# A relation-weighted graph network: the combination bases in chunks of 120 rows instead of 128

## The chip, the cores and the metric

The kernel runs on one core of a Trainium2 chip. The metric is the device time in microseconds of one execution; three runs of the kernel before gave 996.9, 996.52 and 996.86 us, a median of 996.86. One further execution was taken with the hardware profiler.

## The reference, cut to what matters

The whole program is two blocks of a network over 625 nodes with 512 features: graph convolution plus linear attention, then a mixture of experts, then the same again with other layers. The change touches one part only, the weights of the first block's two gated relational convolutions:

```
w = einsum('rb,bio->rio', att, basis)      # r = 2 relations, b = 30 bases, i = o = 512
msg_r = (gate_r * x[col]) @ w[r]           # then chosen by edge type and summed per node
h   = relu(layer1(x)); out = layer2(h)     # each layer has its own basis (30 x 512 x 512) and att (2 x 30)
```

The two bases are 2 x 30 x 512 x 512 fp32 numbers, 62.9 MB. Every output row `w[r, i, :]` is a sum over 30 rows `basis[b, i, :]` with the coefficients `att[r, b]`.

## The kernel before, in words

**The combination.** On the host the bases are laid out in 16 groups (8 for each layer). A group is 64 input rows i: four quarters of 16. For each i the 30 bases follow one another, so a group is 64 x 30 = 1920 rows of 512 numbers, 15 chunks of 128 rows. TensorE multiplies a chunk with a matrix `Am` whose entries are att where a row belongs to the wanted i, and zero elsewhere; the result is 32 rows of 512 (16 values of i for each of two relations), written to one of four quarters of the PSUM bank `CB` (`CB[32 * j:32 * j + 32]`). A quarter is 480 rows, which is 3.75 chunks of 128, so three of the chunks (3, 7 and 11) belong to two quarters and are multiplied twice: 18 products for 15 chunks. `PARTS` lists them as (chunk, quarter), in an order in which four successive ones go to four quarters; `ORDER` is the order of the chunks in memory. Products are fp32.

**The ring.** The 240 chunks come as 80 loads of three chunks (128 rows x 6144 bytes), five loads per group, into seven buffers. SyncE issues them in order (`load_basis`): load n waits until load n-5 has landed and until TensorE has given back the buffer of load n-7. TensorE gives back a buffer after the products number 2, 5, 8, 11 and 17 of a group (`FREES`, semaphore `combo_done`). All loads go through SyncE's one queue.

**The order of the work.** On TensorE a group of products is a call of `combos(n)`. Group 0 and 1 come first, between small products and transposes; then 24 steps of one-hot products follow (`SEGS`, line 497), which count the edges per pair of nodes, with groups 2 to 13 after every second step (`AFTER`); their inputs are made by DVE and ScalarE two steps ahead. After them TensorE computes the root products of layer 1 (line 509), then group 14, a small product that DVE turns into a flag (`many`), and group 15. ScalarE (`combo_out`, even groups) and DVE (`combo_in`, odd groups) take `CB` out to the weights `W`; `combos` waits for that (`w_ready`). Then the stage with the products of line 549 begins, which needs the rounded matrices `Dr` from ScalarE and `GXl` from DVE. When the last group is done, SyncE starts the loads of the next weights (`Wqkv`, `R1`, `R2`).

**Am.** DVE builds it at the start with six operations at line 1226 from a 0/1 mask and att, both loaded before everything else.

Of the kernel before, what the change touches and what calls it, by code (L numbers as in the profile page):

```python
# [29 lines left out]

PARTS = ((0, 0), (4, 1), (8, 2), (12, 3), (1, 0), (5, 1), (9, 2), (13, 3), (2, 0), (6, 1), (10, 2), (14, 3),
         (3, 0), (3, 1), (11, 2), (11, 3), (7, 1), (7, 2))
ORDER = (0, 4, 8, 12, 1, 5, 9, 13, 2, 6, 10, 14, 3, 11, 7)
FREES = (2, 5, 8, 11, 17)
SLOTS = 7

AFTER = [g // 2 + 2 if g % 2 else None for g in range(NS)]
FLUSHES = (NS + PER - 1) // PER  # L40
# [82 lines left out]
def build(nc, A, out):  # L123
    ctx = ExitStack()
    with ctx:
        def sb(name, shape, dt=F32):
            return ctx.enter_context(nc.sbuf_tensor(name, shape, dt))

        def sem(name):
            return ctx.enter_context(nc.semaphore(name))  # L130
# [49 lines left out]
        spare = sb("spare", [128, 3072])  # L180
# [8 lines left out]
        def ar(off, *dims, p=128):  # L189
            n = 1  # L190
            for d in dims:
                n *= d
            v = AR[0:p, off:off + n]
            if len(dims) == 1:
                return v
            names = "abcdefgh"[:len(dims)]
            return v.rearrange("p (%s) -> p %s" % (" ".join(names), " ".join(names)),
                               **{k: d for k, d in zip(names, dims)})

        def sl(i, a, b, p=128):  # L200
            return PS[0:p, i * 1024 + a:i * 1024 + b]
# [9 lines left out]
        def wide(f, o):  # L211
# [6 lines left out]
        oXN, oXT, oG, oZ, oW1, oW2, oR2, oRING, oA, oOT, oB = (  # L218
            0, 2560, 5120, 10240, 15440, 19536, 23632, 25680, 31824, 33872, 40496)
# [12 lines left out]
        W = [ar(oW1, 2, 4, 512), ar(oW2, 2, 4, 512)]  # L232


        Am = ar(oA, 2, 18, 48)
        amask, att = ar(oW2, 18, 16), ar(oW2 + 512, 18, 2, 2)
        ring = [ar(oR2 + 1536 * i, 3, 512) for i in range(5)] + [
            spare[:, 1536 * i:1536 * i + 1536].rearrange("p (c n) -> p c n", c=3) for i in range(2)]
        ei = ar(oOT, 3, EP).bitcast(I32)
        ef = ar(oB + 1024, 3, EP, p=P)  # L240
        ge_ = ar(oOT + 512, NT + 1, EP, p=P)
# [21 lines left out]

        gw = [ar(oB, 2, 512), ar(oB - 374, 2, 512)]
        bias2, bias_out = ar(oB + 512, 512, p=P), ar(oB, 512, p=P)
        R1, R1e = ar(oA, 4, 512), [ar(o, 512) for o in (14720, oRING + 5632, oW2 + 1536, oW2 + 3584)]
        R2 = ar(oR2, 4, 512)
        Wqkv = ar(oRING, 4, 1536)
        WO = ar(oW1 + 2048, 4, 512)
# [1 line left out]
        CB = PS[:, 3584:4096]  # L271
# [9 lines left out]
        d_ring = [sem("d_ring%d" % i) for i in range(5)]  # L281
# [10 lines left out]
        combo_done, seg_done = sem("combo_done"), sem("seg_done")  # L292
# [106 lines left out]
        def _(te):  # L399
            pe = Waits(te)  # L400
# [34 lines left out]
                ins.then_inc(u.sem, 1)  # L435


            def combos(n, a=0, b=len(PARTS)):
                l = n // 8
                pe.wait_ge(w_ready, n)  # L440
                for m, (c, j) in list(enumerate(PARTS))[a:b]:
                    at = ORDER.index(c)
                    pe.wait_ge(d_ring[at // 3], 16 * (n + 1))
                    held = ring[(5 * n + at // 3) % SLOTS]
                    quarter = [k for k, part in enumerate(PARTS) if part[1] == j]
                    ins = te.matmul(CB[32 * j:32 * j + 32, :], Am[:, l, m, 16 * (n % 2):16 * (n % 2) + 32],  # L446
                                    held[:, at % 3, :], start=m == quarter[0], stop=m == quarter[-1])
                    if m in FREES:
                        ins.then_inc(combo_done, 1)

            psum.held.add(3)
            pe.wait_ge(am_ready, 6)
# [26 lines left out]
            for g, (u, v) in enumerate(SEGS):  # L479
# [3 lines left out]
                if first:  # L483
                    for k in range(7):
                        if g:
                            pe.wait_ge(flush_done, NT * (g // PER - 1) + min(NT, (512 * k + 511) // N + 1))
                        te.matmul(PS[0:P, k * 512:(k + 1) * 512], low[0:1, 0:P], low[0:1, 128:640],
                                  start=True, stop=False, skip_group_check=True)
# [3 lines left out]
                for b in range(NT):  # L492
                    with te.If_ne(regs[b], 0):
                        for t in range(u, v):
                            for blk, p0, p1 in PIECES:
                                if blk == b:
                                    te.matmul(PS[0:P, p0:p1], oh_dst(g, t)[:, cols(b)], oh_src(g, t)[:, p0 - b * N:p1 - b * N],  # L497
                                              start=False, stop=False, skip_group_check=True)
# [20 lines left out]
                pe.wait_ge(s, v)  # L519
            for c in range(4):  # L520
                root1(c, bank[c])
            combos(14, 0, 12)
            u = psum.take("many", "dve", slot=2)
            slot(u)
            pe.wait_ge(many_ready, 1)
            te.matmul(sl(u.slot, 0, 10, 1), ones[0:P, 0:1], sm[0:P, 3, 0:2, 0:5], start=True, stop=True).then_inc(u.sem, 1)
            combos(14, 12)
            combos(15)
            psum.at = 2
            psum.held.discard(3)  # L530
# [134 lines left out]
            for c in range(NT):  # L665
                u = psum.take(("l2", c), "dve", slot=c // 2 if c < 4 else None, keep=c in (1, 3))
                o = bank[c] if c < 4 else sl(u.slot, 0, 512, P)
# [60 lines left out]
            for c in range(NT):  # L728
                ins = te.transpose(sl(1, c * P, (c + 1) * P, 8) if c < 4 else sl(1, 512, 512 + P, 8), M[:, c, :], ident[0:P, 0:P])
# [152 lines left out]
            for c in range(NT):  # L882
                read(psum["a1", c])
                o = c * P if c < 4 else 512
                ins = te.transpose(sl(u.slot, o, o + P), x1r[0:P, c, :], ident[0:P, 0:P])
            ins.then_inc(u.sem, 1)
            read(psum["KV", 1, 1])
            for c in range(NT):
# [50 lines left out]
            for c in range(NT):  # L939
                ins = te.matmul(sl(u.slot, c, c + 1, P), x1a[:, cols(c)], wa[:, 1, 0:1], start=True, stop=True)  # L940
# [3 lines left out]
            for c in range(NT):  # L944
                ins = te.transpose(sl(u.slot, c * 128, c * 128 + 128, P), x1a[:, cols(c)], ident[:, :])
# [158 lines left out]
            ins = logits2(4)  # L1104
# [48 lines left out]
        def _(ve):  # L1153
            dv = Waits(ve)
# [68 lines left out]
            dv.wait_ge(d_att, 32)  # L1223
            for lay in range(2):
                for k in range(3):
                    ve.tensor_tensor(Am[:, lay, :, 16 * k:16 * k + 16], amask,
                                     att[:, :, lay, k % 2].unsqueeze(2).to_broadcast([128, 18, 16]),
                                     ALU.mult).then_inc(am_ready, 1)
            dv.wait_ge(d_edge, 16)
            ve.tensor_scalar(nsrc, ei[0:P, 0, :], -STEEP, STEEP / 2, ALU.mult, ALU.add).then_inc(nsrc_ready, 1)  # L1230
# [28 lines left out]
            for i, (b0, b1) in enumerate(((0, 3), (3, 5))):  # L1259
                k = full(("cnt", i))  # L1260
# [24 lines left out]
            def combo_in(k):  # L1285

                l, kc = k // 8, k % 8 // 2
                dv.wait_ge(combo_done, 5 * (k + 1))
                dv.wait_ge(w_ready, k)
                for r in range(2):  # L1290
                    ins = ve.scalar_tensor_tensor(out=W[l][:, r, kc, :], in0=CB, scalar=halves[1 - r], in1=W[l][:, r, kc, :],
                                                  op0=ALU.mult, op1=ALU.add)
                ins.then_inc(w_ready, 1)
# [69 lines left out]
            i = full("many")  # L1363
# [166 lines left out]
            i = full("place", 1)  # L1530
# [22 lines left out]
            for c in range(NT):  # L1553
                ins = ve.tensor_scalar(dgk[:, c, :], ident[0:P, 0:P], key[0:P, c:c + 1], None, ALU.mult)
# [5 lines left out]
            for k in (1, 3):  # L1560
                i = full(("xs", k))
# [3 lines left out]
            i = full("krow")  # L1565
# [208 lines left out]
            for c in range(NT):  # L1774
                i = full(("mo", c))
# [123 lines left out]
            for j in range(2):  # L1899
                i = full(("tp", j))  # L1900
# [31 lines left out]
            for c in range(NT):  # L1932
                i = full(("out", c))
# [4 lines left out]
        def _(se):  # L1938
            ac = Waits(se)
# [45 lines left out]
            def combo_out(k):  # L1985

                l, kc = k // 8, k % 8 // 2
                ac.wait_ge(d_cst, 16)
                ac.wait_ge(combo_done, 5 * (k + 1))
                for r in range(2):  # L1990
                    ins = copy(W[l][:, r, kc, :], CB, scale=halves[r])
                ins.then_inc(w_ready, 1)
# [122 lines left out]
            for k in (0, 2):  # L2115
                i = full(("xs", k))
# [4 lines left out]
            i = full("MT")  # L2121
# [85 lines left out]
            i = full("xt4")  # L2207
# [67 lines left out]
            i = full("x1n")  # L2275
# [187 lines left out]
        def _(ye):  # L2463
            sp = Waits(ye)
# [14 lines left out]
            ye.dma_start(iota[:, :], A["c_iota"]).then_inc(d_iota, 16)  # L2479

            def load_basis(n):
                r = n % 5
                if n >= 5:
                    sp.wait_ge(d_ring[r], 16 * (n // 5))
                if n >= SLOTS:
                    sp.wait_ge(combo_done, n - SLOTS + 1)
                ye.dma_start(ring[n % SLOTS], A["basis"][n]).then_inc(d_ring[r], 16)

            ye.dma_start(X[:, :, :], A["x"].rearrange("c p f -> p c f")).then_inc(d_x, 16)
            ye.dma_start(cst[:, :], A["c_cst"]).then_inc(d_cst, 16)  # L2490
            for n in range(5):
                load_basis(n)
            def load_gates(lay, d):
                ye.dma_start(gw[lay][0:P, :, :].rearrange("p r i -> p (r i)"), A["gate_w"][lay:lay + 1, :].to_broadcast([P, 1024])).then_inc(d, 16)

            load_gates(0, d_gw0)
            for n in range(5, 80):
                load_basis(n)
                if n == 32:
                    for k in range(4):  # L2500
                        ye.dma_start(R1e[k], A["L0_gnn_root1"][128 * k:128 * k + 128, :]).then_inc(d_r1e, 16)
                if n == 40:
                    sp.wait_ge(gl_ready, NT)
                    ye.dma_start(bias1, A["bias1"]).then_inc(d_bias, 16)
                    ye.dma_start(bias2, row(A["L0_gnn_bias2"]).to_broadcast([P, 512])).then_inc(d_bias2, 16)
            sp.wait_ge(combo_done, 80)
            ye.dma_start(Wqkv, kp(A["L0_mix_W_qkv"])).then_inc(d_wqkv, 16)
            ye.dma_start(R1, kp(A["L0_gnn_root1"])).then_inc(d_r1, 16)
            ye.dma_start(R2, kp(A["L0_gnn_root2"])).then_inc(d_r2, 16)
# [157 lines left out]
```

## Time and profile before

| | |
|---|---|
| median of three runs | 996.86 us |
| the profiled execution, its own time | 994.57 us |
| the span of that execution | 992.8 us |
| TensorE matmul busy | 934.3 us, 94% of the span |
| DVE busy | 557.6 us, 56% |
| ScalarE busy | 401.1 us, 40% |
| mean granted TensorE clock | 0.984 of full speed |
| bytes moved by DMA | 124.87 MB, of which 62.9 MB are the bases |

Times in the profile are microseconds from the start of the span unless marked ns. PE is TensorE's matmul part and PEld its weight load part, which overlap; SPq is SyncE's DMA queue. An fp32 product shows as two records. "DMA share" is the mean busy share of the core's 16 DMA engines.

### The profile page before, as it was taken

The page shows a single profiled execution, that of the slowest core. Times are in us where ns is not written, and L with a number is a line of the kernel's source. Part 1 is how long each engine was busy: PE and PEld are TensorE (multiplying, and loading weights), DVE is VectorE, ACT ScalarE, POOL GpSimd, SP SyncE. Part 2 cuts the span into 40 slices and gives each one's busy share as a digit, 9 for nine tenths or more (in the row PEclk, how much of TensorE's full clock was granted, in tenths as well). Part 3 has the DMA queues.
Part 4 walks back from the last instruction along what each step waited for, and adds up shares of the span by engine and source line. Part 5 has one row for each costly group of instructions (what it writes and reads, how often), then busy time and mean ns, then how long its engine had stood idle before and what let it go on. Part 6 is the DMA issues. An engine that isn't in the chain of part 4 may idle for free. (4 is left out here: it accounts for less than half of the span.)

```text
span 992.8 us, 12505 instructions
## 1 busy us (share of the span) xinstructions
PE 934.3 (94%) x4724; PEld 610.9 (62%) x4724; DVE 557.6 (56%) x1176; ACT 401.1 (40%) x670; POOL 109.5 (11%) x98
## 2 busy tenths in 40 slices
PE   3989889999999999999998999989999899999997
PEld 0445444395454494468765656989997644545885
DVE  4798888823147611441315662697876533658861
ACT  3677777311102210111112333478785543424450
POOL 0000000000020213100002000144340000023300
PEclk9999999999999999989999999999999999999899
DMA  9999989560000101062985203222103100230001
GB/s 299 380 392 358 380 332 366 207 218 0 1 21 1 54 20 67 0 223 95 308 288 188 81 1 97 78 64 66 43 1 120 51 1 3 89 85 0 1 1 52
DMA packets 53086, 124.87 MB, mean 126 GB/s; under 512 B 5455, under 2 KB 19539, under 8 KB 53010
## 3 DMA queue, kind: packets, MB, share of 16 engines
q1 hardware_dynamic: 51890, 122.51, 34.6%
q0 software_dynamic: 1120, 1.29, 0.4%
q8 instruction: 56, 0.92, 0.4%
q14 instruction: 20, 0.16, 0.0%
HBM read 120.40 MB, written 3.38 MB: 125 GB/s over the span
## 5 line engine op out<-in xcount | busy, mean ns | idle before, releaser
L412 PE MATMUL PS<-AR 128*125 128x512 f32 (+9 forms) x1394 | 393.9, 440 | 9.0 <-issue 1.9
L412 PEld LDWEIGHTS PS<-AR 128*128 128x128 f32 (+3 forms) x1394 | 212.5, 194 | 168.9 <-issue 161.9
L1951 ACT ACTIVATE AR<-PS 128x500 f32<-128x500 f32 (+6 forms) x73 | 41.9, 578 | 162.4 <-PE PS L412 81.2
L1954 ACT ACTIVATE AR<-iota,AR 125x625 f16<-125x625 f16 x119 | 86.3, 811 | 27.8 <-PE PS L499 27.7
L446 PE MATMUL PS<-AR 128*32 128x512 f32 x420 | 68.1, 628 | 20.8 <-DMA AR<-in_basis 20.5
L1279 DVE TENSOR_SCALAR AR<-iota,AR 125x625 f16<-125x625 f16 x165 | 60.5, 446 | 13.8 <-PE PS L499 13.8
L497 PE MATMUL PS<-AR 125*125 125x512 f16 (+9 forms) x425 | 59.8, 297 | 4.5 <-issue 3.7
L497 PEld LDWEIGHTS PS<-AR 125*125 125x125 f16 x425 | 45.0, 139 | 22.7 <-issue 13.5
L2447 POOL TENSOR_TENSOR whl<-AR,whh 128x512 fp32r<-128x512 f32 x32 | 47.3, 1499 | 90.3 <-ACT whh L1951 90.3
L1799 DVE TENSOR_TENSOR HMl<-AR,HMh 128x626 fp32r<-128x626 f32 x64 | 50.6, 830 | 4.3 <-ACT HMh L1951 4.3
L446 PEld LDWEIGHTS PS<-AR 128*32 128x32 f32 x420 | 15.3, 112 | 57.3 <-issue 39.7
L1951 ACT ACTIVATE HMh<-AR 128x626 fp32r<-128x626 f32 x64 | 43.2, 729 | 13.2 <-DVE AR L1794 13.2
L1954 ACT ACTIVATE sd<-mv,eps 125x1 f32<-125x1 f32 x35 | 10.3, 297 | 94.1 <-DVE mv L1175 86.9
L549 PE MATMUL PS<-Dr,GXh 125*128 125x314 f32 (+1 forms) x160 | 46.7, 310 | 0.0
L549 PE MATMUL PS<-Dr,GXl 125*128 125x314 f32 (+1 forms) x160 | 46.2, 307 | 0.0
L1954 ACT ACTIVATE AR<-PS,bh 128x626 f32<-128x626 f32 (+1 forms) x48 | 35.8, 780 | 18.8 <-PE PS L412 18.7
L1390 DVE TENSOR_SCALAR AR<-PS 125x512 f32<-125x512 f32 (+1 forms) x18 | 13.3, 742 | 50.8 <-PE PS L412 50.8
L412 PE MATMUL PS<-HMh,whh 128*128 128x314 f32 (+1 forms) x128 | 39.8, 311 | 1.8 <-ACT AR L1954 1.5
L412 PE MATMUL PS<-x1h,whh 128*128 128x314 f32 (+1 forms) x128 | 40.1, 313 | 1.1 <-DVE AR L1794 0.8
L412 PE MATMUL PS<-x1h,whl 128*128 128x314 f32 (+1 forms) x128 | 40.1, 313 | 0.0
L412 PE MATMUL PS<-x1l,whh 128*128 128x314 f32 (+1 forms) x128 | 39.4, 308 | 0.0
L412 PE MATMUL PS<-HMl,whh 128*128 128x314 f32 (+1 forms) x128 | 39.3, 307 | 0.0
(320 smaller groups left out, 1512.1 us busy)
## 6 DMA issues: line engine op xcount, KB each, us to landing
AR<-in_basis SPq DMA_DIRECT2D x58, 768.0 KB, 9.4
AR<-in_L_ffn_W SPq DMA_DIRECT2D x20, 1024.0 KB, 7.8
spare<-in_basis SPq DMA_DIRECT2D x22, 768.0 KB, 9.4
AR<-in_L_gnn_Wh SPq DMA_DIRECT2D x8, 512.0 KB, 4.0
AR<-in_L_gnn_Wh SPq DMA_DIRECT2D x16, 256.0 KB, 4.7
AR<-in_L_mix_W_qkv SPq DMA_DIRECT2D x1, 3072.0 KB, 11.4
AR<-in_L_gnn_root SPq DMA_DIRECT2D x2, 1024.0 KB, 14.7
y_dram<-AR SPq DMA_DIRECT2D x8, 256.0 KB, 8.4
```

Source lines behind the costliest of these rows:

```text
L412: ins = te.matmul(o, l, r, start=start and i == 0, stop=stop and i == len(pairs) - 1)
L446: ins = te.matmul(CB[32 * j:32 * j + 32, :], Am[:, l, m, 16 * (n % 2):16 * (n % 2) + 32], held[:, at % 3, :], start=m == quarter[0], stop= ...
L497: te.matmul(PS[0:P, p0:p1], oh_dst(g, t)[:, cols(b)], oh_src(g, t)[:, p0 - b * N:p1 - b * N], start=False, stop=False, skip_group_check=True)
L549: ins = te.matmul(o, w, Dr[r][0:P, d, a:b], **z)
L1279: ve.tensor_scalar(oh_dst(g, t)[:, 0:N], iota[0:P, 0:N], ef[:, 1, t:t + 1], ef[:, 2, t:t + 1], ALU.is_equal, ALU.mult).then_inc(dst_ready, 1)
L1390: ve.tensor_scalar(t, i, 0.0, None, ALU.min).then_inc(phi_min, 1)
L1799: ve.tensor_tensor(HMl[q][:, f, :], tmp[f], f32(HMh[q][:, f, :]), ALU.subtract).then_inc(hm_lo, 1)
L1951: return se.activation(o, i, ACT.Copy, scale=scale)
L1954: return se.activation(o, i, f, bias=bias, scale=scale)
L2447: ge.tensor_tensor(lo[:, ks], v, f32(hi[:, ks]), ALU.subtract).then_inc(pool_wl, 1)
```

## The change

A chunk becomes 120 rows, four values of i with their 30 bases. A quarter is then exactly four chunks, and a group 16 chunks and 16 products, none of them double. A load brings four chunks, one for each quarter: 120 rows of 8192 bytes in SBUF, read from memory as two blocks of 120 rows x 4096 bytes. There are 64 loads, four per group, and five buffers. `Am` has one block of 48 columns per position of the chunk in its quarter (4 instead of 18). Semaphores: one `d_ring` for each buffer, `combo_done` counts four per group, and a load waits only for its buffer. The extra load of `R1e` is issued after load 26 instead of 32, the one of the bias after load 32 instead of 40; one tile of `R1e` moves into what the ring leaves free in `spare`.

```diff
-PARTS = ((0, 0), (4, 1), (8, 2), (12, 3), (1, 0), (5, 1), (9, 2), (13, 3), (2, 0), (6, 1), (10, 2), (14, 3),
-         (3, 0), (3, 1), (11, 2), (11, 3), (7, 1), (7, 2))
-ORDER = (0, 4, 8, 12, 1, 5, 9, 13, 2, 6, 10, 14, 3, 11, 7)
-FREES = (2, 5, 8, 11, 17)
-SLOTS = 7
+ROWS = 120
+LOADS = 64
+SLOTS = 5
...
-        Am = ar(oA, 2, 18, 48)
-        amask, att = ar(oW2, 18, 16), ar(oW2 + 512, 18, 2, 2)
-        ring = [ar(oR2 + 1536 * i, 3, 512) for i in range(5)] + [
-            spare[:, 1536 * i:1536 * i + 1536].rearrange("p (c n) -> p c n", c=3) for i in range(2)]
+        Am = ar(oA, 2, 4, 48, p=ROWS)
+        amask, att = ar(oW2, 4, 16, p=ROWS), ar(oW2 + 512, 2, 2, p=ROWS)
+        ring = [ar(oR2 + 2048 * i, 4, 512, p=ROWS) for i in range(4)] + [
+            spare[0:ROWS, 0:2048].rearrange("p (c n) -> p c n", c=4)]
...
-            def combos(n, a=0, b=len(PARTS)):
+            def combos(n, a=0, b=4):
                 l = n // 8
                 pe.wait_ge(w_ready, n)
-                for m, (c, j) in list(enumerate(PARTS))[a:b]:
-                    at = ORDER.index(c)
-                    pe.wait_ge(d_ring[at // 3], 16 * (n + 1))
-                    held = ring[(5 * n + at // 3) % SLOTS]
-                    quarter = [k for k, part in enumerate(PARTS) if part[1] == j]
-                    ins = te.matmul(CB[32 * j:32 * j + 32, :], Am[:, l, m, 16 * (n % 2):16 * (n % 2) + 32],
-                                    held[:, at % 3, :], start=m == quarter[0], stop=m == quarter[-1])
-                    if m in FREES:
-                        ins.then_inc(combo_done, 1)
+                for j in range(a, b):
+                    m = 4 * n + j
+                    pe.wait_ge(d_ring[m % SLOTS], 16 * (m // SLOTS + 1))
+                    for q in range(4):
+                        ins = te.matmul(CB[32 * q:32 * q + 32, :], Am[:, l, j, 16 * (n % 2):16 * (n % 2) + 32],
+                                        ring[m % SLOTS][:, q, :], start=j == 0, stop=j == 3)
+                    ins.then_inc(combo_done, 1)
...
-                    ve.tensor_tensor(Am[:, lay, :, 16 * k:16 * k + 16], amask,
-                                     att[:, :, lay, k % 2].unsqueeze(2).to_broadcast([128, 18, 16]),
+                    ve.tensor_scalar(Am[:, lay, :, 16 * k:16 * k + 16], amask, att[:, lay, k % 2:k % 2 + 1], None,
                                      ALU.mult).then_inc(am_ready, 1)
...
             def load_basis(n):
-                r = n % 5
-                if n >= 5:
-                    sp.wait_ge(d_ring[r], 16 * (n // 5))
+                r = n % SLOTS
                 if n >= SLOTS:
                     sp.wait_ge(combo_done, n - SLOTS + 1)
-                ye.dma_start(ring[n % SLOTS], A["basis"][n]).then_inc(d_ring[r], 16)
+                ye.dma_start(ring[r].rearrange("p (h c) n -> p h c n", h=2), A["basis"][n].rearrange("h p c n -> p h c n")).then_inc(d_ring[r], 16)
```

## Rows read from the trace of the kernel before

**Rows 1.** The page, busy tenths of 40 equal slices of the span.
```profile
PE   3989889999999999999998999989999899999997
...
DMA  9999989560000101062985203222103100230001
```

**Rows 2.** DMA issues of the whole execution: count, KB each, median us to landing.
```profile
AR<-in_basis SPq DMA_DIRECT2D x58, 768.0 KB, 9.4
...
spare<-in_basis SPq DMA_DIRECT2D x22, 768.0 KB, 9.4
```

**Rows 3.** Windows: length, busy us of each engine, clock, DMA share, GB/s.
```profile
12.00:36.00 24.00, 17.97 (x84) 5.18 (x84) 14.79 (x44) 9.51 (x16) 0.00 (x0) 0.86 1.02 368
36.00:72.00 36.00, 33.10 (x238) 16.39 (x238) 30.89 (x85) 25.81 (x38) 0.00 (x0) 1.00 0.98 383
72.00:84.00 12.00, 10.36 (x77) 6.04 (x77) 11.34 (x32) 9.31 (x14) 0.00 (x0) 1.00 0.76 300
84.00:144.00 60.00, 54.04 (x389) 30.21 (x388) 50.44 (x121) 45.71 (x66) 0.00 (x0) 0.97 1.01 391
144.00:156.00 12.00, 11.76 (x102) 6.74 (x101) 10.73 (x26) 8.38 (x12) 0.00 (x0) 1.00 0.58 211
156.00:180.00 24.00, 23.41 (x143) 10.43 (x142) 21.12 (x37) 15.90 (x26) 0.00 (x0) 1.00 1.01 400
180.00:192.00 12.00, 10.63 (x62) 3.47 (x65) 10.95 (x30) 2.37 (x5) 0.00 (x0) 1.00 0.45 153
...
168.00:180.00 12.00, 11.47 (x41) 4.43 (x34) 12.00 (x18) 7.40 (x13) 0.00 (x0) 1.00 1.00 413
```

**Rows 4.** TensorE's timeline: start, us, work, idle before it, releaser.
```profile
14.38 5.37 PE L446 MATMUL PS<-AR 128*32 128x512 f32 x18 [14.38 <-DMA AR<-in_basis]
...
23.72 1.94 PE L446 MATMUL PS<-AR 128*32 128x512 f32 x8 [2.31 <-DMA AR<-in_basis]
...
36.56 1.92 PE L446 MATMUL PS<-AR 128*32 128x512 f32 x12 [0.83 <-DMA AR<-in_basis]
...
101.09 1.92 PE L446 MATMUL PS<-AR 128*32 128x512 f32 x12 [0.82 <-DMA AR<-in_basis]
...
171.17 13.97 PE L509 MATMUL PS<-AR 128*125 128x512 f32 x32 [0.21 <-DVE AR L1329]
...
190.95 1.48 PE L446 MATMUL PS<-spare,AR 128*32 128x512 f32 x10 [1.37 <-ACT AR L1951]
...
195.59 1.92 PE L446 MATMUL PS<-AR 128*32 128x512 f32 x12 [0.80 <-DMA AR<-in_basis]
197.44 0.42 PE L549 MATMUL PS<-Dr,GXh 125*128 125x314 f32 x1
```

**Rows 5.** Timeline of SyncE's queue, then of ScalarE, before 198 us.
```profile
186.22 2.01 SPq L2487 DMA_DIRECT2D AR<-in_basis  x3
...
191.30 6.25 ACT L1951 ACTIVATE Dr<-AR 125x626 fp32r<-125x626 f32 x10
```

**Rows 6.** Timeline of TensorE in group 3: a weight load, the products.
```profile
54.75 0.15 PEld L446 LDWEIGHTS PS<-AR 128*32 128x32 f32 x4 [0.27 <-issue]
...
54.32 2.78 PE L446 MATMUL PS<-AR 128*32 128x512 f32 x24 [0.34 <-issue]
56.90 1.92 PE L446 MATMUL PS<-spare,AR 128*32 128x512 f32 x12
```

**Rows 7.** Windows: the last three loads; the second gate load.
```profile
187.00:195.00 8.00, 6.40 (x46) 1.28 (x38) 6.16 (x15) 5.37 (x10) 0.00 (x0) 1.00 0.83 296
281.00:284.00 3.00, 3.00 (x29) 3.00 (x28) 2.14 (x9) 0.00 (x0) 0.00 (x0) 1.00 0.32 130
```

**Rows 8.** TensorE's waits, 36 to 198 us; one in its timeline.
```profile
PE PS L446 <- DMA AR<-in_basis: 2.7, 4, 0.8
...
PE PS L446 <- DMA spare<-in_basis: 0.3, 1, 0.3
...
130.29 2.09 PE L497 MATMUL PS<-AR 125*125 125x173 f16 x14 [2.28 <-issue]
```

More of the change, by code:

```diff
@@ L265, in build @@
         bias2, bias_out = ar(oB + 512, 512, p=P), ar(oB, 512, p=P)
-        R1, R1e = ar(oA, 4, 512), [ar(o, 512) for o in (14720, oRING + 5632, oW2 + 1536, oW2 + 3584)]
+        R1, R1e = ar(oA, 4, 512), [
+            ar(14720, 512), spare[:, 2048:2560], ar(oW2 + 1536, 512), ar(oW2 + 3584, 512)]
         R2 = ar(oR2, 4, 512)
@@ L521, in _ @@
                 root1(c, bank[c])
-            combos(14, 0, 12)
+            combos(14, 0, 3)
             u = psum.take("many", "dve", slot=2)
@@ L526, in _ @@
             te.matmul(sl(u.slot, 0, 10, 1), ones[0:P, 0:1], sm[0:P, 3, 0:2, 0:5], start=True, stop=True).then_inc(u.sem, 1)
-            combos(14, 12)
+            combos(14, 3)
             combos(15)
@@ L1287, in combo_in @@
                 l, kc = k // 8, k % 8 // 2
-                dv.wait_ge(combo_done, 5 * (k + 1))
+                dv.wait_ge(combo_done, 4 * (k + 1))
                 dv.wait_ge(w_ready, k)
@@ L1988, in combo_out @@
                 ac.wait_ge(d_cst, 16)
-                ac.wait_ge(combo_done, 5 * (k + 1))
+                ac.wait_ge(combo_done, 4 * (k + 1))
                 for r in range(2):
@@ L2481, in load_basis @@
             def load_basis(n):
-                r = n % 5
-                if n >= 5:
-                    sp.wait_ge(d_ring[r], 16 * (n // 5))
+                r = n % SLOTS
                 if n >= SLOTS:
                     sp.wait_ge(combo_done, n - SLOTS + 1)
-                ye.dma_start(ring[n % SLOTS], A["basis"][n]).then_inc(d_ring[r], 16)
+                ye.dma_start(ring[r].rearrange("p (h c) n -> p h c n", h=2), A["basis"][n].rearrange("h p c n -> p h c n")).then_inc(d_ring[r], 16)
             ye.dma_start(X[:, :, :], A["x"].rearrange("c p f -> p c f")).then_inc(d_x, 16)
             ye.dma_start(cst[:, :], A["c_cst"]).then_inc(d_cst, 16)
-            for n in range(5):
+            for n in range(SLOTS):
                 load_basis(n)
@@ L2496, in _ @@
             load_gates(0, d_gw0)
-            for n in range(5, 80):
+            for n in range(SLOTS, LOADS):
                 load_basis(n)
-                if n == 32:
+                if n == 26:
                     for k in range(4):
                         ye.dma_start(R1e[k], A["L0_gnn_root1"][128 * k:128 * k + 128, :]).then_inc(d_r1e, 16)
-                if n == 40:
+                if n == 32:
                     sp.wait_ge(gl_ready, NT)
@@ L2505, in _ @@
                     ye.dma_start(bias2, row(A["L0_gnn_bias2"]).to_broadcast([P, 512])).then_inc(d_bias2, 16)
-            sp.wait_ge(combo_done, 80)
+            sp.wait_ge(combo_done, LOADS)
             ye.dma_start(Wqkv, kp(A["L0_mix_W_qkv"])).then_inc(d_wqkv, 16)
@@ L2631 @@
     a["basis"] = np.stack([g["L0_gnn_basis1"], g["L0_gnn_basis2"]])[:, :, group].transpose(0, 2, 3, 1, 4).reshape(
-        16, 15, 128, 512)[:, list(ORDER)].reshape(80, 3, 128, 512).transpose(0, 2, 1, 3)
-    flat = 128 * np.array([c for c, _ in PARTS])[None, :] + np.arange(128)[:, None]
-    a["att"] = np.stack([g["L0_gnn_att1"], g["L0_gnn_att2"]])[:, :, flat % 30].transpose(2, 3, 0, 1)
-    a["c_amask"] = (flat[:, :, None] // 30 == np.arange(16) + 16 * np.array([j for _, j in PARTS])[:, None]).astype(np.float32)
+        16, 2, 2, 4, ROWS, 512).transpose(0, 3, 1, 4, 2, 5).reshape(LOADS, 2, ROWS, 2, 512)
+    rows = np.arange(ROWS)
+    a["att"] = np.stack([g["L0_gnn_att1"], g["L0_gnn_att2"]])[:, :, rows % 30].transpose(2, 0, 1)
+    a["c_amask"] = (4 * np.arange(4)[:, None] + rows[:, None, None] // 30 == np.arange(16)).astype(np.float32)
     a["gate_w"] = np.stack([g["L0_gnn_gate_w1"], g["L0_gnn_gate_w2"]]).reshape(2, 1024)
```

## Prediction

> **What bounds the kernel now.** I read the page's 40 slices first, then the DMA share by stage, then TensorE's own timeline of the stage the change touches, then SyncE's. The reader is to see in [rows 1] that TensorE is busy nearly everywhere, and that in the first eight slices (some 198 us), unlike the rest, the DMA engines are full too. That stage reads the 62.9 MB of bases (80 loads of 768 KB, [rows 2]) while TensorE works through 16 groups of combination products, with the one-hot products between them. [Rows 3] is the ledger of that stage: between 36 and 180 us the 16 engines are full in all but two stretches, at 383 to 400 GB/s, 392 in the mean; the free time is 24% of 12 us around 78 us (2.9 us) and 42% of 12 us around 150 us (5.0 us). Both are places where the ring was full because TensorE came late to a group. So the stage stands on two legs of nearly one length: TensorE alone would need little less, the DMA engines alone would need 7.9 us less. [Rows 4] show which leg carries: TensorE stood still for a load in groups 1, 7, 13 and 15 (0.83, 0.82, 0.3 and 0.80 us, that of group 13 in [rows 8]). In these four groups a later load is a later end, one for one. After 197.44 us the next stage starts at once on TensorE, and what else it needs is there: the rounding of Dr began at 191.30 and was at its tenth and last tile at the end [rows 4, 5]. A shift at 197 us goes through to the end.
>
> **The change, part by part.**
>
> *Products.* A group now has 18 products in five rounds; those of a round lie in different quarters of the output and run side by side. [Rows 6]: weight loads come four at a time every 0.43 us, twice per product (fp32 is recorded as two), so a round is 0.86 us whatever its number of products, and a group is 10 x 0.43 = 4.3 us (54.32 to 58.82 with its ends, 4.5). After the change it is four rounds of four: 3.44 us. That is 0.86 us less TensorE work per group, 13.8 us over sixteen. Rows 120 instead of 128 deep don't change a pass. Whether it counts is the loads' matter.
>
> *Loads.* 80 x 786,432 bytes become 64 x 983,040: the same 62.9 MB. What changes is who carries them. A load to 128 rows keeps 16 engines full [rows 3]. The nearest row for another number of rows is the second gate load, 125 rows of 4096 bytes, alone on the queue: a DMA share of 0.32 at 130 GB/s [rows 7]. That is five engines of 16 (5/16 = 0.31), each at 130/5 = 26 GB/s. 125 rows are five times 25. I take it that the rows are dealt in equal shares to at most 16 engines, so 120 rows go to 15 engines, eight rows each, and one stands idle.
> The Trainium skill says the same ("DMA: Bandwidth & Descriptors", section "Why a DMA increments its semaphore by 16 and not by 1"): the number of engines is the largest one up to 16 that divides the slowest dimension of both sides, 10 for 100 partitions. By that rule it is 15 for 120. It speaks against this change, and this trace agrees for 125 rows.
> Packet size: 26 GB/s per engine at 4096 bytes stands beside 413/16 = 25.8 at 6144 bytes in the fullest stretch (168 to 180 us, [rows 3]). I cost the smaller packets at nothing; at most 2% of the stream (3 us) if their fixed part is paid more often, and 3 us less if 15 engines meet fewer delays than 16 (392 is 95% of 413). So 62.9 MB take 62.9/392 = 160.5 us now and 171.2 us at 15/16 of it: +10.7 us, bounds +7 and +14. Up to group 13, 14 of 16 groups: +9.4 us (6 to 12).
>
> *Ring.* Now 7 buffers of 3 chunks, 21 chunks of 128 rows (5.5 MB); then 5 of 4, 20 of 120 rows (4.9 MB). The 0.6 MB that can't be held ahead are 1.5 us of the stream: of the 7.9 us of free DMA time some 6 us remain to soak up the slower stream (bounds 3 and 7.9). In its place the last load of a group releases less work: now two rounds follow it (1.85 us from the last wait, 195.59 to 197.44, [rows 4]), then one (0.86): -1.0 us.
> Up to the end of group 13: 9.4 - 6.0 - 1.0 = +2.4 us.
>
> *End of the stage.* Between groups 13 and 14 TensorE has 13.97 us of root products [rows 4]; meanwhile the ring fills and the queue stands (share 0.45 from 180 to 192, [rows 3]). The time from there is set by what can't be in the ring yet. Now 7 of the last 10 loads are in it and three follow; the first is issued at 186.22, a round after group 14 began [rows 5]; data flow in the 8 us from 187 at 296 GB/s, 2.37 MB [rows 7], and the last product pair waits until 195.59. After: five of eight are in the ring, and three of 0.98 MB follow, 2.95 MB. At 296 x 16/15 us per byte: 8.0 x 1.25 x 1.067 = 10.7 us against 8.0, +2.7 by this row; of the 8 us one is start and end, so I take 2.35. The last rounds save 0.9. Together +1.45 us (bounds +0.5, +2.5). The wait of 1.37 us for ACT between groups 14 and 15 [rows 4] lies before this and is covered: group 14 ends 0.86 earlier, and TensorE waits for loads instead.
>
> *Small edits.* Am is built by six DVE operations, which shrink from 288 elements to 64; but the first product waits for its load, until 14.38 [rows 4], not for them: nothing. The mask and att loads shrink with them. The five first loads go out with no wait, 4.9 MB instead of 3.9, and the gate load behind them lands later, which some 0.5 us of the bounds hold; the first group only needs the first load, 0.2 MB longer: 0.5 us, part of the stream. R1e's second tile moves to another place, and the loads at n = 26 and 32 stand at the same byte of the stream as 32 and 40 did. 32 fewer products are 128 fewer records of 12,505: nothing.
>
> **Sum.** +2.4 + 1.45 = +3.85 us. TensorE also lost 2.3 us before 130.29 to neither a load nor an engine that the profile names [rows 8]; arriving later, it may lose less of such time. I take 0.4 off: +3.4 us. The profiled span goes from 992.8 to 996.2, its own time from 994.57 to 998.0; the shown runs have a median 2.3 us above that one (996.86), so the median goes to **1000.3 us**. Its own range, by the bounds (+7 instead of +10.7 in the stream and all 7.9 us soaked up; +14 and 3 us): 997 to 1007.
>
> **Rivals.**
> *A, the loads keep all 16 engines (or 15 move as much).* 64 loads of 240 packets deal evenly, 15 to an engine, if packets and not rows are dealt; and 15 x 26 = 390 GB/s is what 16 reach now with their delays. Against it: the 125-row load has 125 packets, and its five engines don't tell rows from packets; but it shows that uneven counts are not dealt to 16. Then the shorter groups count: 12 x 0.86 = 10.3 us for TensorE in groups 2 to 13, of which the stream gives no more than its free 7.9, less some 2 for the smaller ring: -6. At the end 0.59 MB more after the ring (+2.0) and 0.9 less work: +1. Together -5: 992 us, at best 989. This is the side of faster.
> *B, the slack is wider than I think.* TensorE waited for loads in only 2.7 + 0.3 us after 36 us [rows 8]. If the free time soaks up all (7.9) and the stream loses but 7, group 13 ends 1 to 2 us earlier and the end gives it back: 0 to +2, 997 to 999 us.
> *C, the 15 engines get in one another's way.* With eight rows in a row each, two engines may come to write the same part of the memory at once; 128 rows on 16 engines evidently don't (25.8 GB/s each). If such pairs share one engine's rate half of the time, the stream of 171 us becomes 1.5 times as long: +85 us less 6 of slack, some 1080 us; if all the time, 1165. It decides as soon as the rate falls below 360 GB/s. For it speaks nothing in this trace; against it, five engines at full rate with 125 rows [rows 7], but few engines rarely meet.
> The Trainium skill ("SBUF — State Buffer", section "Door 1: The DMA port swizzle (why `[64,N]` ≈ `[32,N]`)") has partitions 32 apart behind one port, each port at one engine's rate; by it engines e and e+4 would meet. No row here shows it.
> *D, TensorE's clock.* After a wait of 2.31 us before 23.72 [rows 4] the granted clock was lower (0.86 in the mean of 12 to 36 us, [rows 3], so partly at 1.2 instead of 2.4 GHz). More waits for loads may bring more of it; while loads set the pace it costs nothing, and 1 to 2 us at most in the groups that TensorE sets. It widens the range only.
>
> **How the numbers follow.** The forecast case +1.5 to +10 has 0.52; A 0.22; B 0.14; C 0.12. 0.2% is 2.0 us, about what a measurement of this kernel tells from no change. Faster: A, and a little of B: 0.24. Same: most of B and the low end of the forecast: 0.20. Slower: 0.56. The range from 990 to 1008 us holds A, B and nearly all of the forecast; C is left out.
>
> **What would show it.** The DMA share in the full stretches falls to 0.94 (15/16) and GB/s to about 365 to 370; packets of 4096 bytes, and L446 with 512 records. TensorE's L446 rounds: 8 steps of 0.43 us per group when all is there. The waits of L446 for loads rise from 3 us after 36 us to about 15, one before the last round in most groups; the DMA share around 78 and 150 us rises. Next stage from 197.44 to about 200.8. A share of 1.0 at 390 GB/s and a stage end near 192 is A; a share of 0.94 with 200 to 300 GB/s is C. Wrong in another way I would be if the stages after 197 us changed their length by more than 1 us.

## The result, and the profile after

| | before | after |
|---|---|---|
| median | 996.69 us (4 runs, 993.92 to 996.9) | 1098.56 us (4 runs, 1098.06 to 1111.89) |
| the profiled execution, its own time | 994.57 us | 1098.57 us |
| its span | 992.8 us | 1096.8 us |
| mean granted TensorE clock | 0.984 | 0.934 |

The ratio is 1.1061 [1.0976, 1.1147]: the changed kernel is slower by a tenth, some 100 us, where 1000.3 us was forecast.

In the changed kernel line 444 holds the combination products, 494 and 496 the one-hot products, 546 the first products of the next stage and 2481 the loads. First the page's slices, as in [rows 1]. A slice is now 27.4 us.

```profile
PE   1576757777699999999999989999999999999998
...
PEclk9786866888799999999899999999999999999899
DMA  8989999999750001020439750051210400230001
GB/s 205 239 224 212 225 216 230 250 237 251 169 188 1 4 16 49 2 77 1 167 121 316 266 200 1 0 159 39 78 39 1 153 1 3 79 77 1 1 1 47
```

In the first ten slices the DMA engines are nearly as full as before and move 205 to 251 GB/s. The stage takes almost eleven slices, and TensorE is idle in a third of it (busy 191.0 of 299.3 us). The issues, as in [rows 2] (count, KB, median us to landing):

```profile
AR<-in_basis SPq DMA_DIRECT2D x52, 960.0 KB, 18.1
```

A load of 1.25 times the bytes needs twice the time. By stretch, as in [rows 3] (length, busy us of each engine, clock, DMA share, GB/s):

```profile
36.00:72.00 36.00, 24.26 (x141) 10.74 (x140) 19.14 (x60) 15.79 (x23) 0.00 (x0) 0.72 0.90 245
72.00:84.00 12.00, 5.34 (x35) 1.37 (x32) 8.31 (x25) 6.42 (x10) 0.00 (x0) 0.93 0.97 207
84.00:144.00 60.00, 38.28 (x225) 21.02 (x229) 29.67 (x75) 25.80 (x37) 0.00 (x0) 0.76 0.98 218
...
192.00:240.00 48.00, 34.33 (x219) 16.14 (x217) 35.17 (x81) 27.87 (x41) 0.00 (x0) 0.85 0.97 244
```

From 84 to 144 us the share is 0.98 at 218 GB/s, where it was 1.01 at 391. The share alone would say that nothing happened; share and rate together say that the engines are busy and slow. TensorE's timeline, as in [rows 4] and [rows 6] (start, us, work, idle before it, releaser):

```profile
18.18 1.94 PE L444 MATMUL PS<-AR 120*32 120x512 f32 x8 [18.18 <-DMA AR<-in_basis]
22.63 1.93 PE L444 MATMUL PS<-AR 120*32 120x512 f32 x8 [2.51 <-DMA AR<-in_basis]
27.17 1.94 PE L444 MATMUL PS<-AR 120*32 120x512 f32 x8 [2.60 <-DMA AR<-in_basis]
...
65.49 1.06 PE L444 MATMUL PS<-AR 120*32 120x512 f32 x8 [0.33 <-issue]
66.34 1.07 PE L444 MATMUL PS<-spare,AR 120*32 120x512 f32 x8
67.20 1.93 PE L444 MATMUL PS<-AR 120*32 120x512 f32 x16
69.06 1.25 PE L494 MATMUL PS<-AR 125*125 125x512 f16 x7
...
297.48 1.93 PE L444 MATMUL PS<-AR 120*32 120x512 f32 x8 [2.57 <-DMA AR<-in_basis]
299.34 0.63 PE L546 MATMUL PS<-Dr,GXh 125*128 125x314 f32 x1
```

At the start a load lands every 4.54 us (22.63 to 27.17): 983,040 bytes in 4.54 us are 217 GB/s. TensorE waits for a load before each of the first rounds, and before 29 of the 64 in all. The next stage begins at 299.34 instead of 197.44: +101.9 of the 104.0 us between the two profiled executions. The other 2.1 us lie behind it. The waits, as in [rows 8], but from 12 to 302 us (total, times, longest):

```profile
PE PS L444 <- DMA AR<-in_basis: 79.2, 24, 18.2
PE PS L444 <- DMA spare<-in_basis: 13.0, 5, 3.2
```

The longest, 18.2 us, is the wait for the first load, which was 14.38 us before [rows 4].

### The profile page after: what moved, and what is told of

The parts are those of the page before. It is cut to its first block and busy times, and to the rows that moved or that the text cites. A ratio compares the mean times of both kernels' runs of the same rounds, so it can differ in the third digit from the quotient of the medians.

```text
span 1096.8 us, 12288 instructions
## 1 busy us (share of the span) xinstructions
PE 961.6 (88%) x4660; PEld 618.8 (56%) x4660; DVE 556.4 (51%) x1176; ACT 401.0 (37%) x670; POOL 109.5 (10%) x98
## 5 line engine op out<-in xcount | busy, mean ns | idle before, releaser
L444 PE MATMUL PS<-AR 120*32 120x512 f32 x416 | 71.4, 767 | 84.8 <-DMA AR<-in_basis 79.2
L444 PEld LDWEIGHTS PS<-AR 120*32 120x32 f32 x416 | 10.9, 119 | 128.5 <-DMA AR<-in_basis 94.2
L494 PE MATMUL PS<-AR 125*125 125x512 f16 (+9 forms) x425 | 73.6, 341 | 5.7 <-issue 4.7
L494 PEld LDWEIGHTS PS<-AR 125*125 125x125 f16 x425 | 54.7, 165 | 32.2 <-issue 22.8
L1950 ACT ACTIVATE AR<-PS,bh 128x626 f32<-128x626 f32 (+1 forms) x48 | 35.8, 780 | 18.4 <-PE PS L411 18.2
L411 PE MATMUL PS<-HMh,whl 128*128 128x314 f32 (+1 forms) x128 | 39.3, 307 | 0.0
## 6 DMA issues: line engine op xcount, KB each, us to landing
AR<-in_L_gnn_root SPq DMA_DIRECT2D x2, 1024.0 KB, 14.9
```

The source lines that it names most:

```text
L411: ins = te.matmul(o, l, r, start=start and i == 0, stop=stop and i == len(pairs) - 1)
L444: ins = te.matmul(CB[32 * q:32 * q + 32, :], Am[:, l, j, 16 * (n % 2):16 * (n % 2) + 32], ring[m % SLOTS][:, q, :], start=j == 0, stop=j == 3)
L1950: return se.activation(o, i, f, bias=bias, scale=scale)
```

## The experiments

Theory P from the start was rival C of the prediction: rows that lie 32 apart (within 0 to 63, or within 64 to 127), and close neighbours, share one way into SBUF (an entry), one engine's rate wide. The rival theories were the smaller packets (Q), the changed order of products and ring, and any number of engines other than 16 (N). A median is given where there was more than one run; the others are single runs beside kernels of the same chip.

### Loads alone, rows and packets varied (p1_loads_alone)

```
for rows in 128, 120, 112, 96, 64:       # 8 loads of two packets of 4096 bytes a row, then one wait
    T[0:rows, i, 0:2048] <- basis
128 and 120 rows x 8192 bytes, x 6144 bytes; ten rows that lie 1, 4, 8, 12 apart; 128 and 120 rows back to memory
```

> Only loads (and two sets of stores), sets of eight, each set waited for; zeros are written as output, the computation is left out. Theory P (engines that hold neighbouring rows come in pairs to one part of SBUF): 128 rows move at 390 to 420 GB/s, whatever the packets (4096, 6144, 8192 bytes); 120 rows at 215 to 250 GB/s, whatever the packets; ten rows on ten engines at 10 x 25 = 250 GB/s when they lie 12 partitions apart, at a quarter to a third of it when adjacent, four partitions apart between these two, eight apart about half. Theory Q (packets of 4096 bytes or the two blocks in memory are the cause): 120 rows in packets of 8192 or 6144 bytes are fast (370 GB/s and more), 128 rows in packets of 4096 bytes slow. Theory N (any number of engines other than 16 is slow): 112 and 96 rows, on 16 engines, at 390 and more; ten rows alike whatever their distance.

Windows of this program, each inside one set, in the order 128, 120, 112, 96, 64 rows; 128 and 120 rows x 8192 bytes; ten rows 1, 4, 8 and 12 apart; stores of 128 and 120 rows. The last two numbers are DMA share and GB/s.

```profile
4.00:20.00 16.00, 0.00 (x0) 0.00 (x0) 1.00 1.03 413
27.00:58.00 31.00, 0.00 (x0) 0.00 (x0) 1.00 0.96 217
66.00:86.00 20.00, 0.00 (x0) 0.00 (x0) 1.00 1.03 288
93.00:113.00 20.00, 0.00 (x0) 0.00 (x0) 1.00 1.03 246
121.00:136.00 15.00, 0.00 (x0) 0.00 (x0) 1.00 1.03 206
143.00:158.00 15.00, 0.00 (x0) 0.00 (x0) 1.00 1.01 425
166.00:197.00 31.00, 0.00 (x0) 0.00 (x0) 1.00 0.95 212
...
251.00:265.00 14.00, 0.00 (x0) 0.00 (x0) 1.00 0.68 69
272.00:280.00 8.00, 0.00 (x0) 0.00 (x0) 1.00 0.61 132
284.00:293.00 9.00, 0.00 (x0) 0.00 (x0) 1.00 0.66 124
297.00:302.00 5.00, 0.00 (x0) 0.00 (x0) 1.00 0.56 182
308.00:322.00 14.00, 0.00 (x0) 0.00 (x0) 1.00 1.02 421
330.00:346.00 16.00, 0.00 (x0) 0.00 (x0) 1.00 0.94 384
```

The disputed cost stands by itself: 120 rows move at 217 GB/s with nothing else running, the rate inside the kernel, and 128 at 413. One packet of 8192 bytes instead of two of 4096 changes little (212 and 425). Theory N falls: 112 and 96 rows keep all 16 engines busy (share 1.03) and move 288 and 246. The way out of SBUF has no such loss: 384 is 421 x 15/16 within 3%.

Ten rows side by side move 69 GB/s, 2.6 engines' worth by ten engines (share 0.68 for 10/16). No two of them are 32 apart, so close neighbours share an entry too. Eight apart, where pairs are 32 apart, they move 124, near the half that P had; four apart, which P had between these two, they move 132. 12 apart, where they are neither neighbours nor 32 apart, they move 182, and P had 250. The windows of this set are short and not quite full (share 0.56), and why it stays low is open.

### The changed kernel with whole rows as one packet (k1_one_packet_of_8192)

```diff
-ye.dma_start(ring[r].rearrange("p (h c) n -> p h c n", h=2), A["basis"][n].rearrange("h p c n -> p h c n"))
+ye.dma_start(ring[r], A["basis"][n])                    # a load's 120 rows x 8192 bytes stand whole in memory
```

> The changed kernel with each row of a load as one packet of 8192 bytes instead of two of 4096. P: nothing gained, 1085 to 1110 us, DMA share 0.94 to 0.97 at 215 to 250 GB/s. Q: 990 to 1005 us.

1112.95 us beside 995.65 for the kernel before on this chip. The same stretch as above:

```profile
84.00:144.00 60.00, 41.70 (x237) 20.98 (x234) 34.55 (x90) 29.09 (x42) 0.00 (x0) 0.78 0.96 220
```

220 GB/s: packets are not the cause. The time is 3 us above the upper end of P's range.

### The kernel before with 120 of 128 rows (k2_before_120_rows)

```diff
-ye.dma_start(ring[n % SLOTS], A["basis"][n])
+ye.dma_start(ring[n % SLOTS][0:120], A["basis"][n][0:120])     # and the products read 120 rows
```

> The kernel before with one thing changed: each load brings, and each product uses, 120 of the 128 rows; the last eight rows of every chunk are left out of the sums. Ring, packets of 6144 bytes, 18 products and order stay. P: the stage becomes as slow as in the changed kernel though 6% less is loaded: 59 MB at 220 to 245 GB/s, 1070 to 1095 us. Q, or the ring of five as the cause: 985 to 1000 us.

1079.74 us beside 995.65, with 6% fewer bytes than before:

```profile
84.00:144.00 60.00, 45.12 (x265) 21.79 (x258) 31.15 (x80) 27.26 (x41) 0.00 (x0) 0.81 0.97 226
```

The old packets (6144 bytes), ring (seven) and products (18) are all there. The row count alone makes the slow stream.

### The changed kernel, loads filled up to 128 rows (k3_padded_to_128)

```diff
-ring = [ar(oR2 + 2048 * i, 4, 512, p=ROWS) for i in range(4)] + ...
+ring = [ar(oR2 + 2048 * i, 4, 512) for i in range(4)] + ...
+a["basis"] = np.concatenate([a["basis"], a["basis"][:, :, 0:128 - ROWS]], axis=2)   # the products read 120 rows
```

> The changed kernel with loads of 128 rows, of which products use 120; 8 rows are loaded for nothing (67.1 MB in place of 62.9), packets of 4096 bytes, ring of five, 16 products stay. P: 16 engines at full rate, 67.1 MB at 392 GB/s = 171 us, so 995 to 1003 us. Q or the ring as the cause: 1080 us and more.

1006.89 us (9 runs), ratio 1.0118 [1.0085, 1.0150] to 995.65 (12 runs).

```profile
84.00:144.00 60.00, 52.06 (x375) 28.89 (x373) 51.09 (x127) 45.55 (x67) 0.00 (x0) 0.94 0.98 375
```

With eight useless rows per load, 6.7% more bytes (67.1 MB), nine tenths of the loss are gone. All other parts of the change (16 products, the ring of five, the small edits) are in this kernel, so together with the extra bytes they cost 11 us in the net (8.5 to 14.9 by the interval). That is 4 us above the upper end of P's range. This is the best of the new forms, and it is still 1.2% slower than before.

### The same rows in other partitions (p2_same_rows_elsewhere)

```
8 loads of two packets of 4096 bytes a row:
64 rows at 0, at 32, at 64; 32 at 0, at 48; 120 at 8; 60 at 0, at 36; 126 at 0; 80 at 0; 120 as 64 at 32 + 32 at 0 + 24 at 96
```

> Only loads in sets of eight (packets of 4096 bytes), zeros as output. Theory P, in its sharp form: an engine carries an equal share of neighbouring rows, and partitions p and p+32 (not p+64) lie behind one port that passes one engine's rate. It then gives, from 26.4 GB/s per port: 64 rows at partition 0 or 64: 206 to 215 GB/s, the same 64 rows at partition 32: 400 to 415; 32 rows at 0 and at 48: 205 to 215; 120 rows at partition 8: 200 to 220; 60 rows at 0: 200 to 220, at 36: 370 to 396; 126 rows (14 engines, nine rows each, so that pairs don't meet): 345 to 370; 80 rows at 0: 200 to 215. Rival: the number of rows alone sets the rate, wherever they lie: 64, 60 and 120 rows the same at every place, 126 rows below 250.

Windows, in the order 64 rows at 0, 32, 64; 32 rows at 48; 120 at 8; 60 at 0 and at 36; 126 at 0:

```profile
4.00:20.00 16.00, 0.00 (x0) 0.00 (x0) 1.00 1.03 210
26.00:34.00 8.00, 0.00 (x0) 0.00 (x0) 1.00 0.99 355
42.00:56.00 14.00, 0.00 (x0) 0.00 (x0) 1.00 1.03 206
...
75.00:80.00 5.00, 0.00 (x0) 0.00 (x0) 1.00 1.03 206
88.00:119.00 31.00, 0.00 (x0) 0.00 (x0) 1.00 0.96 211
126.00:142.00 16.00, 0.00 (x0) 0.00 (x0) 1.00 0.96 192
148.00:154.00 6.00, 0.00 (x0) 0.00 (x0) 1.00 0.95 371
162.00:180.00 18.00, 0.00 (x0) 0.00 (x0) 1.00 0.90 353
```

This is the run that names the mechanism. The same 60 rows with the same packets move 192 GB/s at 0 and 371 at 36; 64 rows move 210 at 0 and 355 at 32 (418 to 420 from 30 to 34 us, once they are under way). Rows 32 to 95 hold no two rows that are 32 apart on one side of 64; rows 0 to 63 hold nothing but such pairs. So p and p + 32 on one side of 64 share an entry. If 64 rows are dealt to 16 engines as four neighbours each, then four neighbours side by side with the next four don't meet (420 at 32), and each engine of rows 0 to 63 meets one other: eight entries, 206/8 = 26 GB/s each, which is one engine's rate.

32 rows at 48 hold no pair 32 apart, and yet move 206. With two rows to an engine, two engines stand within four neighbours. So an entry serves some four neighbouring rows and the four that lie 32 above; the ten neighbouring rows of the run before fit that too (10/4 entries x 26 = 65 GB/s, an estimate, for 69 measured).

The rival (the number of rows alone) falls with 60 and 64 rows. Two of P's ranges were missed: 60 rows at 0 were below theirs (192 for 200 to 220), and 80 rows above (226 for 200 to 215).

The Trainium skill ("SBUF — State Buffer", section "Door 1: The DMA port swizzle (why `[64,N]` ≈ `[32,N]`)") has a map of 16 ports in which four neighbouring partitions and the four 32 above share one port, and these rows agree with it. Its section "Can I just issue two DMAs to hit both halves?" says that only a transfer over all 128 partitions reaches all 16 ports; there 64 rows at partition 32 differ, with 355 GB/s in the window and up to 420 in its later part.

### A ring with one buffer less (k4_before_ring_of_six)

```diff
-SLOTS = 7
+SLOTS = 6
```

> The kernel before with SLOTS = 6 in place of 7: loads of 128 rows, 18 products and 62.9 MB stay; what the ring holds beyond one group falls from 6 chunks to 3. If the ring's room is what the padded kernel still lacks (its room beyond a group is 4 chunks of 16): +4 to +8 us, 1000 to 1005. If the room counts for little and the padded rows are its whole loss: 995 to 998.

1000.24 us (10 runs), ratio 1.0051 [1.0030, 1.0072] to 996.31 (13 runs): one buffer of 0.79 MB is worth 3 to 7 us. The median lies at the low end of the range for the ring's room.

### Quarters in chunks of 128, 128, 128 and 96 rows (k5_quarters_as_128_128_128_96, k6_tail_as_64_and_32)

```diff
-ye.dma_start(ring[r], A["basis"][n])                           # 120 rows
+ye.dma_start(ring[r][0:ROWS[n % 4]], A["basis"][n][:, 0:ROWS[n % 4]])       # k5; ROWS = (128, 128, 128, 96)
+for a, b in ((0, 128),) if n % 4 < 3 else ((32, 96), (0, 32)): ...          # k6: the 96 rows as two loads
```

> The changed kernel with the four chunks of a quarter cut as 128, 128, 128 and 96 rows: 16 products, ring of five, no padding, 62.9 MB. P with the rates of the loads alone: 3.15 MB of a group at 413 GB/s and 0.79 MB at 246 are 10.8 us against 10.2 of the padded kernel, so 1010 to 1020 us. If bytes counted alone: 994 to 1000.

> The same cut, but the 96 rows come as 64 rows at partition 32 and 32 rows at partition 0. P: 0.52 MB at 413 and 0.26 MB at 206 GB/s are 2.5 us in place of 3.2, the group 10.2 us, as in the padded kernel: 1001 to 1009 us. If place doesn't matter: as the run before or slower for its 16 further loads, 1012 to 1025.

1043.56 and 1023.1 us beside 996.31. The stretch from 84 to 144 us of the first, then of the second:

```profile
84.00:144.00 60.00, 46.30 (x288) 26.11 (x280) 44.20 (x111) 40.77 (x60) 0.00 (x0) 0.85 0.97 290
```

```profile
84.00:144.00 60.00, 49.89 (x317) 30.55 (x319) 41.20 (x106) 37.34 (x55) 0.00 (x0) 0.84 0.96 309
```

The order is as P has it: where the same 96 rows lie and how they are cut is worth 20 us, by one run of each. Both sizes are misses. By the rates of the loads alone the first should stream at 1/(0.8/391 + 0.2/246) = 350 GB/s; it reached 290. This mixed stream is slower than its parts, and why was not found.

### The kernel before with 126 rows (k7_before_126_rows)

The edit is that of k2, with 126 for 120. Alone, 126 rows moved 353 GB/s, so P in its simple form promised nearly the old time.

> The kernel before with loads and products of 126 of the 128 rows; the last two rows of every chunk are left out of the sums. 126 rows go to 14 engines of nine rows, which lie 36 partitions apart and so don't meet. P: DMA share 0.88 and 340 to 360 GB/s in the full stretches; 61.9 MB need 175 us instead of 158, less some of the free time: 1004 to 1016 us, some 70 us faster than with 120 rows although one engine less works. Rival (any load that is not of 128 rows is as slow as that of 120): 1070 to 1095 us.

1078.5 us beside 994.14: P's range was missed, the rival's was hit.

```profile
36.00:72.00 36.00, 25.27 (x138) 9.23 (x139) 19.81 (x59) 16.82 (x23) 0.00 (x0) 0.81 0.89 256
...
84.00:144.00 60.00, 46.44 (x255) 23.57 (x257) 30.46 (x80) 29.37 (x43) 0.00 (x0) 0.74 0.90 236
```

The share of 0.90 says 14 engines (14/16 is 0.88, and full is 1.01 to 1.03 in these views), nine rows each. If the rows are dealt as equal shares of neighbours, engines e and e + 4 are 36 rows apart, not 32: they need the same entry only in part, and only if one is ahead of the other. That gave theory P2: 126 rows are fast while the engines run in step.

### In step, and with five engines put behind (p3_five_engines_behind)

```
16 loads, without and with one load ahead of them in the queue that nobody waits for:
D[0:125, 0:1024] <- basis                                     # 125 rows x 4096 bytes: five engines, 25 packets each
126 rows at 0; 60 at 36; 128; 120 (with only); 126 rows x 6144 bytes
```

> Leaves out the whole computation: sets of 16 loads from the bases, each set waited for before the next, and zeros as output. Sets: 126 rows from partition 0 (two packets of 4096 bytes a row); the same with one load of 125 rows x 4096 bytes queued ahead of it and not waited for, which occupies only engines 0 to 4 (25 packets each, some 4 us) and so puts these five behind the others; 60 rows from partition 36, without and with that load ahead; 128 rows, without and with; 120 rows with it; 126 rows x 6144 bytes as in the kernel with 126 rows, without and with. Theory P2 (partitions 32 apart share a port, and the rate depends on whether the engines that share are at it at the same moment; 126 rows are fast only while the engines run in step): 126 rows 340 to 370 GB/s without and 215 to 255 with the load ahead, at both packet sizes; 60 rows from 36 stay fast, 350 to 370 without and 310 to 350 with (its own engines wait out the 4 us); 128 rows 395 to 415 without and 370 to 405 with; 120 rows 180 to 210. Rival Q (the packet of 6144 bytes, with rows that are not next to one another in memory, is what made the kernel with 126 rows slow): 126 rows x 4096 stay at 340 to 370 with and without, 126 rows x 6144 are at 225 to 255 in both sets. Rival R (the computing engines at work beside the loads make it slow): all four sets of 126 rows are at 330 to 370.

Windows: 126 rows alone; with the load ahead, its first 8 us and the rest; 60 rows at 36 with it; 128 rows with it, once its 4 us have passed; 120 rows with it; 126 rows x 6144 bytes alone; with it, after its first 8 us.

```profile
4.00:44.00 40.00, 0.00 (x0) 0.00 (x0) 1.00 0.90 355
52.00:60.00 8.00, 0.00 (x0) 0.00 (x0) 1.00 0.90 246
60.00:104.00 44.00, 0.00 (x0) 0.00 (x0) 1.00 0.90 305
...
140.00:158.00 18.00, 0.00 (x0) 0.00 (x0) 1.00 0.96 350
...
226.00:250.00 24.00, 0.00 (x0) 0.00 (x0) 1.00 1.03 410
262.00:320.00 58.00, 0.00 (x0) 0.00 (x0) 1.00 0.96 220
340.00:372.00 32.00, 0.00 (x0) 0.00 (x0) 1.00 0.89 312
...
392.00:424.00 32.00, 0.00 (x0) 0.00 (x0) 1.00 0.89 300
```

One small load ahead takes 126 rows from 355 to 246 GB/s for 8 us and to 305 for the rest of the set, with no compute engine at work (rival R falls) and with packets of 4096 bytes (rival Q falls as the only cause). A part of the 246 is the small load itself: with 128 rows behind it, the four us from 212 show 249 GB/s too. But 128 rows then come back to 410, and 60 rows at 36 to 390 (392 without the load), while 126 rows, once behind, never come back to 355. That is what P2 has for engines out of step.

The sizes of P2 were in part wrong: after 8 us the rate settled at 305 instead of staying under 255; packets of 6144 bytes ran at 312 with nothing ahead of them, which P2 had at 340 to 370; and 120 rows with the load ahead moved 220 where it had at most 210. That a load ahead costs 126 rows a lasting 50 GB/s is shown; that it does so by the step of the engines is argued, since no trace tells the engines apart. What keeps 126 rows at 230 to 256 throughout the kernel, where each load is issued by itself when a buffer comes free, is not shown, nor is the part that the packet of 6144 bytes has. A like reason, neighbouring loads that are dealt to the engines in different ways, could explain the low rates of k5 and k6, but no run tried that.

## Why the prediction was wrong, by its own steps

**Loads: the step that failed.** It had 120 rows go to 15 engines, and each keep 26 GB/s. The first half fits the trace: the share fell from 1.01 to 0.97 or 0.98 in most full stretches, and 1.01 x 15/16 is 0.95. The second half was wrong: 218/15 is 14.5 GB/s per engine. The term of the sum, 62.9 MB at 367 GB/s, was 171.2 us; at the 207 to 247 GB/s of the windows it is 255 to 304. The rate of five engines with 125 rows [rows 7] was carried over to 15. That five engines of 25 rows each need no common entry for long is argued; the prediction itself said that few engines rarely meet.

That 120 rows halve the rate is shown three times (p1, k2, and k3 the other way round). How the shared entries make 217 GB/s of it is argued. If each engine has eight neighbouring rows, engines e and e + 4 need the same two entries. If both always want the same one at the same time, eight entries of 26 GB/s work at once, which is 208. But they could take turns, and a load put ahead of them, which might have parted them, changed nothing (220). And eight neighbouring rows for each of 16 engines would make the same pairs out of 128 rows, which moved 413. So 128 rows must be dealt to the engines in another way, or something else is at work too. No run here shows how either is dealt.

**Rival C: right in its mechanism and its sign, given 0.12.** Its price for pairs that meet half of the time, 1080 us, was near; the stream became 367/218 = 1.68 times as long, not 1.5. The range, which ended at 1008 us, left it out. Its test, a share of 0.94 with 200 to 300 GB/s, is about what the trace shows (0.97 or 0.98 in most stretches, 0.90 in one). Nothing in the trace of before excluded it: the only rows on the question were for 128 rows, where 16 engines evidently don't hinder one another (25.8 GB/s each), and for five engines. That an unknown is not shown was read as that it is unlikely.

**Products: right.** A group is four rounds, 3.57 us from 65.49 to 69.06 against 3.44 and its ends. It saved nothing that can be seen, because loads set the pace.

**Packet size: right at nothing** for the changed kernel: 218 GB/s with 4096 bytes, 220 with 8192 (k1). What 6144 bytes do with 126 rows is open (p3).

**Ring and free time: probably mis-sized too.** 0.6 MB of room were put at 1.5 us of the stream. In the kernel before 0.79 MB are worth 3 to 7 us (k4). k3 shows what the forecast would have met without rival C, because its stream is as long as the one forecast: 67.1 MB at 391 GB/s are 171.6 us instead of 160.9, +10.7. The sum had +3.4 us for the whole change; k3 was +11.2 (1006.89 to 995.65). So the free DMA time, of which 6 us were to soak up the slower stream, did little in the net. How the loss divides between it, the smaller ring and the extra bytes was not separated. (The mean of the full stretches of [rows 3] is 390 GB/s, not 392, which is worth 0.6 us.)

**End of the stage: the shorter tail didn't come.** The last load releases one round instead of two, forecast at 0.86 us instead of 1.85. It took 1.86 us (297.48 to 299.34). The clock says why:

```profile
297.00:299.00 2.00, 1.52 (x8) 0.20 (x8) 0.00 (x0) 0.00 (x0) 0.00 (x0) 0.50 0.00 0
```

0.50 is 1.2 GHz; TensorE had waited 2.57 us just before. It is so in the middle of the stage too: the round at 103.48 took 1.94 us after a wait of 3.19 us, where a round at full clock takes 1.06.

```profile
103.00:105.00 2.00, 1.52 (x8) 0.20 (x8) 0.56 (x2) 0.00 (x0) 0.00 (x0) 0.50 0.97 215
```

The rounds at 22.63 and 27.17 took 1.93 us as well, but there the profile has the granted clock at 1.00, so what slowed them is not shown. Rival D's remark, that more waits bring more low clock and that it costs nothing while loads set the pace, holds but for this last round. TensorE's busy time rose by 27.3 us (934.3 to 961.6) with fewer products.

**The stages after** were to keep their length within 1 us. They took 2.1 us more. Some 0.7 us of it lie at their start: the first products of line 546 ran at the low clock (0.63 and 0.46 us where 0.31 us is usual). The rest is not traced to a cause. It isn't simply the starved stage before them, for k3 begins them at the low clock too and takes as long for all of them as the kernel before (795.35 us).

## What to carry to other kernels

Read the DMA share together with GB/s: a nearly full share at half the rate was the sign here that the engines hinder one another, and no wait in the trace named it. Before changing the number of rows of a stream that bounds a kernel, time the loads alone in the new shape and place: a program with no computation (p1) gave 217 GB/s, where the whole kernel had 218. A row count that divides the work more neatly can cost more than the padding (1.012 with eight useless rows against 1.106 without). A rate measured for few engines is no price for many: where the trace has no row for the new shape and one known mechanism could halve the rate, give that case its full chance.

## What the runs showed of the hardware

- Into SBUF the rate depends on which rows are written. Rows p and p + 32 on one side of 64, and some four neighbouring rows, share an entry of about 26 GB/s. Alone: 128 rows 413 GB/s, 126 rows 353, 120 rows 217, 112 rows 288, 96 rows 246, 64 rows 206 to 210 at 0 and 355 (later 420) at 32, 60 rows 192 at 0 and 371 at 36, 32 rows at 48 206.
- Out of SBUF 120 rows lost only the idle engine: 384 GB/s, 128 rows 421.
- The rate of 126 rows depends on what went before: 355 GB/s alone, 246 just behind a small load to 125 rows, 305 later, 230 to 256 in the stretches of a kernel. 128 rows and 60 rows at 36 come back to their full rate (410, 390) behind the same load.
- Cutting the load didn't help: 120 rows as 64 at 32, 32 at 0 and 24 at 96 moved 222 GB/s. Whether other cuts, or parts from two queues, bring 120 rows to the full rate was not tried.
